# One decoder layer on one core: the hand-written order of every engine laid out anew

## What is computed

```python
# 1. linear attention with decay, 32 heads of 16
h = layernorm(x); xx = shifted(h) - h
r, k, v = (h + xx*maa_r) @ Wr.T + br, ..., ...
g = silu((h + xx*maa_g) @ Wg.T + bg)
y = ((r @ k) * Wm) @ v + (r @ state) * wb       # per head
x = x + ((headnorm(y) * ln_g + ln_b) * g) @ Wo.T + bo
# 2. cross attention: queries layernorm(x), keys and values ctx, 32 query and 8 key heads
x = x + softmax(q @ k.T / 4) @ v
# 3. feed-forward; every operand of both matmuls is rounded to 8 bits with one exponent per block of 32
h = mx_layernorm(bf16(layernorm(x)))
h = gelu(mx_quant(h) @ mx_quant(W1).T + b1)
x = x + bf16(residual + (mx_quant(h) @ mx_quant(W2).T + b2))
```

## Time and profile before

| what | value |
|---|---|
| median of 3 runs | 1534.97 us (1533.75 to 1541.5) |
| the profiled execution's own time | 1538.03 us |
| its span, first to last instruction | 1536.0 us |
| TensorE busy | 1297.9 us, 84% |
| VectorE busy | 1265.8 us, 82% |
| ScalarE busy | 773.2 us, 50% |
| GpSimd busy | 559.9 us, 36% |
| TensorE busy tenths, 40 slices of 38.4 us | 0004999999999999999999999999999999998743 |
| VectorE busy tenths | 3676647878899999999999998999999899887664 |
| granted clock of TensorE, mean | 0.974 |

### The profile page before, as it was taken

The page is one execution under the profiler, slowest core; times in us unless marked ns, Lnnn a source line. Parts: engine busy times, 40 slices in busy tenths (PEclk is TensorE's granted clock), DMA queues, the critical chain, the costliest instruction groups (busy, mean ns, idle before and its releaser), DMA issues.

```text
span 1536.0 us, 30462 instructions
## 1 busy us (share of the span) xinstructions
PE 1297.9 (84%) x11493; PEld 826.9 (54%) x11552; DVE 1265.8 (82%) x2092; ACT 773.2 (50%) x1611; POOL 559.9 (36%) x606
## 2 busy tenths in 40 slices
PE   0004999999999999999999999999999999998743
PEld 0003666556666666666666665666666666665311
DVE  3676647878899999999999998999999899887664
ACT  2002457556555555555555555665555555554340
POOL 2224333333344444443433343333444443433111
PEclk9999999999999999999999999999999999999766
DMA  7542000111111111111111111111111111111112
GB/s 284 121 98 47 9 8 14 35 36 33 26 36 34 27 23 27 35 34 35 34 34 34 35 34 34 34 34 28 34 35 22 21 35 34 35 32 29 25 25 44
DMA packets 150831, 62.76 MB, mean 41 GB/s; under 512 B 137632, under 2 KB 139040, under 8 KB 149920
## 3 DMA queue, kind: packets, MB, share of 16 engines
q1 hardware_dynamic: 150688, 60.83, 17.5%
HBM read 26.73 MB, written 8.39 MB: 23 GB/s over the span
## 4 chain that ended last, share of the span: by engine, by line
PE 32%; DVE 31%; issue 14%; DMA 9%; SPq 7%; ACT 6%; POOL 1%; DVEq 0%; POOLq 0%; ACTq 0%
PE bank_b L396 9%; DMA xin<-x 5%; PE rt L454 4%; SPq L214 4%; DVE att L1327 4%; DMA gmem<-w 3%; PE bank_y L419 2%; PE bank_o L480 2%; DVE amax_g L1400 2%; DVE mix_v L1304 2%; SPq L208 2%; PE bank_b L489 2%; PE bank_a L489 2%; PE bank_a L396 1%; PE rt L444 1%
## 5 line engine op out<-in xcount | busy, mean ns | idle before, releaser
L2880 POOL TENSOR_TENSOR x<-x,o_bf 128x512 f32<-128x512 f32 x32 | 37.2, 1162 | 488.6 <-DVE o_bf L1477 488.6
L1327 DVE TENSOR_TENSOR att<-rt,wm 128x2048 f32<-128x2048 f32 x64 | 146.3, 2286 | 5.1 <-PE bank_y L419 3.0
L1361 DVE TENSOR_REDUCE negm<-rt 128x16 f32<-128x2048 f32 x64 | 146.3, 2287 | 3.6 <-PE rt L454 2.1
L378 PE MATMUL bank_o<-ident,xx 128*128 128x128 f32 x128 | 20.4, 283 | 144.1 <-ACT xx L2244 143.6
L2875 POOL TENSOR_TENSOR gmem<-gmem,unit_g 128x1024 bf16<-128x1024 bf16 x64 | 124.5, 1945 | 47.2 <-DVE unit_g L1411 46.1
L500 PE MATMUL bank_y<-w2q,gmem 128*128 128x512 bf16 x511 | 118.9, 387 | 17.9 <-DMA gmem<-gmem 16.9
L2342 ACT ACTIVATE pT<-rt 128x2048 f32<-128x2048 f32 x64 | 119.5, 1868 | 14.1 <-PE rt L467 11.7
L396 PE MATMUL bank_b<-mix_k,w_Wk 128*128 128x128 f32 x1024 | 123.1, 280 | 3.5 <-DVE mix_k L1304 3.5
L396 PEld LDWEIGHTS bank_b<-mix_k,w_Wk 128*128 128x128 f32 x1024 | 121.4, 197 | 7.1 <-issue 3.8
L396 PE MATMUL bank_a<-mix_r,w_Wr 128*128 128x128 f32 x1024 | 122.6, 278 | 0.0
L433 PE MATMUL bank_y<-w_Wo,yT 128*128 128x512 f32 x256 | 120.5, 614 | 0.0
(11 more groups left out here) (171 smaller groups left out, 2938.1 us busy)
## 6 DMA issues: line engine op xcount, KB each, us to landing
xin<-x SPq DMA_DIRECT2D x32, 256.0 KB, 3.2
gmem<-w SPq DMA_DIRECT2D x16, 512.0 KB, 4.5
out<-x SPq DMA_DIRECT2D x32, 256.0 KB, 2.0
kv<-ctx SPq DMA_DIRECT2D x32, 64.0 KB, 3.1
w_Wv<-Wv SPq DMA_DIRECT2D x1, 1024.0 KB, 5.7
w_Wk<-Wk SPq DMA_DIRECT2D x1, 1024.0 KB, 8.6
w_Wr<-Wr SPq DMA_DIRECT2D x1, 1024.0 KB, 12.7
w_Wg<-Wg SPq DMA_DIRECT2D x1, 1024.0 KB, 14.8
```

The costliest lines, as they stand in the source:

```text
L1327: e.tensor_tensor(att[:, :, :, :, :].rearrange("p g m a t -> p (g m a t)"), rt[:, :], wm[:, i, :, :, :, :].rearrange("p g m a t -> p (g m ...
L1361: e.tensor_reduce(negm[:, 0:H].rearrange("p (g i j) -> p g i j", g=4, i=2)[:, :, i, :], rt[:, :].rearrange("p (g j s) -> p g j s", g=4, j= ...
```

## The change

Nothing that is computed changes but one thing: the gate's bias is added by ScalarE in four instructions (`gate_in`, a function of ScalarE now) and not by VectorE in one. Everything else is order. The 16 weight pieces stand between the steps of the first four sequences on VectorE, GpSimd and SyncE; the first loads come in another order; the loops run over `range(9, 28)` with another order inside, and the written-out starts and ends differ from before in many places.

```diff
@@ SyncE, the first loads
+            load_w12(0)
             load("Wv", wt["Wv"][:, :, :], weights["Wv"])
             load("dist", minus_dist, consts["minus_dist"])
             load("bv", row["bv"][:, :], rows["bv"])
...
             load_w12(1)
...
             load("b1", b1row[:, :], b1)
             for k in ROWS[1:]:
                 load("rows", row[k][:, :], rows[k])
+            load_x(1)
+            load("Wk", wt["Wk"][:, :, :], weights["Wk"])
+            load("faaaa", bonus[:, :], faaaa)
+            load("Wo", headmean[:, :], consts["headmean"])
+            load("Wo", wt["Wo"][:, :, :], weights["Wo"])
+            load("Wr", wt["Wr"][:, :, :], weights["Wr"])
+            load("Wg", wt["Wg"][:, :, :], weights["Wg"])
+            w12_turned(0)
             load_w12(2)
+            load_w12(3)
+            load_w12(4)
             w12_turned(1)
...
@@ VectorE
-            def gate_in(n):
+            def gate(n):
                 e.wait_ge(sem("act_gt"), n + 1)
-                if n:
-                    e.wait_ge(sem("dve_yT"), n)
-                e.tensor_tensor(gh[:, :, :], heads4(bank_b[:, :]), per_col(col["bg"]), ALU.add).then_inc(sem("dve_gh"), 1)
-
-            def gate(n):
-                e.wait_ge(sem("dve_gh"), n + 1)
+                e.wait_ge(sem("act_gh"), n + 1)
...
@@ ScalarE
+            def gate_in(n):
+                e.wait_ge(sem("pe_g"), n + 1)
+                if n:
+                    e.wait_ge(sem("dve_yT"), n)
+                for m in range(KT):
+                    done = e.activation(gh[:, m, :], bank_b[:, m * T:(m + 1) * T], ACT.Identity,
+                                        bias=col["bg"][:, m:m + 1])
+                done.then_inc(sem("act_gh"), 1)
...
@@ GpSimd, from the start
             w12_scaled(0)
+            mixed(0, "r")
             w12_scaled(1)
+            mixed(0, "g")
             w12_scaled(2)
+            mixed(1, "g")
+            mixed(1, "r")
             w12_scaled(3)
             w12_scaled(4)
+            gate_parts(0)
+            gate_rstd(0)
...
```

More of the change, by code:

```diff
@@ new lines, in _ @@
+            e.wait_ge(sem("dve_Ra1"), 27)
+            scores_x(25, 0)
+            e.wait_ge(sem("act_neg"), 26)
+            head_variance(26)
+            e.wait_ge(sem("act_rz"), 28)
+            project_v(27)
+            e.wait_ge(sem("act_ex0"), 26)
+            scores_x(25, 1)
+            e.wait_ge(sem("act_expv"), 53)
+            values_x(25, 0)
+            e.wait_ge(sem("dve_yz"), 27)
+            project_out(26)
+            e.wait_ge(sem("act_ex1"), 26)
+            scores_r(27, 0)
@@ L1551, in _ @@
+            stats_q(2)
+            spread_v(1)
+            norm_mv("q", 2)
+            w12_scale(8)
+            decayed(1, 1)
             w12_quantise(7)
-            means_removed()
-            w12_scale(8)
+            w12_quantise(8)
+            differences(2)
+            mixed(2, "k")
             w12_scale(9)
-            w12_quantise(8)
+            maxima(0, 0)
+            w12_scale(10)
             w12_quantise(9)
-            w12_scale(10)
+            maxima(0, 1)
+            gate(1)
@@ L2637, in _ @@
+            weights_x(25, 0)
+            keys_r(27)
             out_x(25, 0)
```

1767 lines of the change are left out of this document (861 added, 906 removed).

## The result

The changed kernel takes 1512.15 us (median of 4 runs, 1510.58 to 1513.42) against 1535.77 for the kernel before: a ratio of 0.984, 95% interval 0.9811 to 0.9869. It is faster, but by 24 us and not by the 67 forecast, and it lies outside the range of 1440 to 1496.

The account below looks back on a forecast made before the run. The prediction took the start to be bound by a chain of loads and VectorE's work, the loop by TensorE. 1538.0 - 53.6 (start) - 13.5 (loop) = 1470.9, with gate and drain 0; 1468 after 3.1 for median runs; range 1440 to 1496.

Parts of the forecast that it names:

- The start: Up to sequence 3, weight pieces between the sequences' steps: head_variance(3) 53.6 us earlier, at 223.
- The waits for the pieces' loads: VectorE in the start: 9 us at piece 2, 25 us over pieces 5 to 15 and what follows; before, 37.0.
- Rival A: In the start, the weight pieces stay a chain: 36 us gained there, 1485 us in all; chance 0.22 together with B.
- Rival B: In the start, TensorE runs at a slow clock: another 15 us, 1483 in all; chance 0.22 together with A.
- The gate: gate_in moved from VectorE to ScalarE: covered by other work, 0 us; up to 1.1 a sequence if not.
- The loop: Sequences 4 to 31: TensorE's waits shrink, 0.5 us faster a sequence, 13.5 us over 27 periods.
- The waits for `pT` and `xx`: TensorE in the loop, before the second scores_x and turn_x: 0.4 and 0.3 us a sequence, both should go.
- `mix_v` is free of GpSimd's product: VectorE in the loop: the mix of v took 2.8 us beside GpSimd's gmem multiplication, which is now done elsewhere.
- `down`: TensorE in the loop: starts 1 us earlier after project_out, three turnings still in a row; near zero, either sign.
- Rival E: In the loop, a smaller loss of D's kind, 1.1 us a sequence: 1511 us; chance 0.07.
- D: In the loop, the mix of r comes late, project("r") 2.3 us late each turn: 1543 us; chance 0.03.
- The drain: The last 110 us, from the last head_variance: keeps its chain, 0 us.

Follow-up runs that it names:

- e5_quant: The changed kernel with VectorE's gelu_quantised(.,0) back behind hidden_quantised in the loop, as in the kernel before: 1484.8 us.
- e3_turn: The changed kernel with SyncE turning the gelu's first half ahead of the hidden in the loop: 1483.5 us.
- e2_early: The changed kernel with gelu_pow2(.,1) back right behind gelu_max(.,1) in the loop, and GpSimd's gelu_scale(.,1) ahead of gate_rstd again: 1511.8 us.

## Why the prediction was right and wrong

**The start: right.** `decayed(3, 0)` was put at 194.3 and came at 191.2, `head_variance(3)` at 223 and came at 220.5; 53.6 us were forecast, 56.2 came. Its parts were less good. The waits for the pieces' loads were 16.6 us, where I had 29 (34 with the load of sequence 3 and `weighted(0)`), while waits that I had not named in the list took their place: 7.0 for the load of sequence 2 and some 14 for other engines, where I had allowed 10. So the sum came out near partly because its terms missed in opposite ways. The quantising of a piece was slowed beside GpSimd more rarely than before, and not more often as I had feared: of the even pieces the median is 1.23 us (the row below) and not 2.0, and of all 16 pieces 3 took over 1.9 us where 7 had. Rival A is out: the pieces are no chain. Rival B is out as a price: the granted clock was 0.88 up to the mark, between the two levels, and the mark still came early.

```profile
L1489 DVE SCALAR_TENSOR_TENSOR hz<-gmem,pow_w x8: 1224/1226/2817, 13.1 to 175.2; 128x1024 bf16<-128x1024 f32 x8
```

**The gate: right at 0 for the kernel before, wrong for this one.** In the old order the move is worth 3.8 us, near my 0. In the new one the same half on VectorE would stand between weight steps and hold `project("k")` of sequence 1 for 14.2 us. So some 18 of the start's 56 us hang on the gate, a term that I had put at 0. I costed the edits one by one against the old order, and they are not independent. How much of it is the place that I gave `gate_in` in that list was not tried.

**The loop: wrong, and this is the step that failed.** I wrote "I take 0.5 faster, nearer to the row of waits". It came 1.65 slower: 13.5 us were to be gained over 27 turns and 43.8 were lost over 28. I had read the waits of TensorE, seen that each could go, and taken what was left as a gain. The waits for `pT` and `xx` did go, though `turn_x` kept a wait of 0.3 us for another reason. What I had not done is walk VectorE's stretch from `second_out` to `yT`, as I had walked its list at the start. Here is its start, each wait in it and its end, first before, then after, in one turn of each:

```profile
746.58 0.68 DVE L1470 SCALAR_TENSOR_TENSOR o_bf<-bank_y,r_b 128x512 bf16<-128x512 f32 x1
...
748.52 0.98 DVE L1297 TENSOR_TENSOR xx<-xT 128x512 f32<-128x512 f32 x1 [0.20 <-ACT xT L2280]
...
753.00 0.26 DVE L1367 RECIPROCAL rden<-bank_o 128x16 f32<-128x16 f32 x1 [0.15 <-PE bank_o L480]
...
771.15 0.75 DVE L1395 SCALAR_TENSOR_TENSOR hz<-hw,rstd_g,r_ffn_ln_b 128x512 bf16<-128x512 f32 x1 [0.30 <-ACT rstd_g L2232]
...
773.99 0.69 DVE L1348 TENSOR_TENSOR yT<-yT,gh 128x512 f32<-128x512 f32 x1
```

```profile
751.06 0.68 DVE L1465 SCALAR_TENSOR_TENSOR o_bf<-bank_y,r_b 128x512 bf16<-128x512 f32 x1
...
753.50 1.22 DVE L1395 TENSOR_REDUCE amax_g<-gmem 128x32 f32<-128x1024 bf16 x1 [0.70 <-ACT gmem L2347]
...
755.60 0.42 DVE L1370 TENSOR_TENSOR x<-bank_o,rden 128x256 f32<-128x256 f32 x1 [0.36 <-DMA out<-x]
...
757.40 0.69 DVE L1297 TENSOR_TENSOR xx<-xT 128x512 f32<-128x512 f32 x1 [0.18 <-ACT xT L2261]
...
768.01 2.29 DVE L1327 TENSOR_TENSOR att<-rt,wm 128x2048 f32<-128x2048 f32 x1 [0.92 <-PE rt L406]
...
780.71 0.69 DVE L1343 TENSOR_TENSOR yT<-yT,gh 128x512 f32<-128x512 f32 x1
```

From the first start to the last end it is 28.1 us before (774.68 - 746.58) and 30.3 after (781.40 - 751.06). The waits are 0.65 before and 2.16 after, 1.5 more; work is 0.7 more, with `gelu_round` and `gelu_quantised` of the first half in it (1.45 us) and `gate_in` out of it. Before, TensorE came to `project_out` some 0.9 us after `yT` was there; that cover went first. The rest is TensorE's wait. That this stretch and the row of turnings set the turn, in rings that close from one turn to the next, is what `e5_quant` and `e3_turn` show: 1.3 and 1.5 us a turn back, each by one edit on one of the two.

My one argument for a gain there, that `mix_v` is free of GpSimd's product, was true (2.79 to 1.14 us), and the 1.7 us came back on `pow_h`. I had written that "GpSimd now does that multiplication elsewhere" and not asked where. `e2_early` shows that another place within the stretch is no better. The Trainium skill ("SBUF — State Buffer", section "SBUF: two separate sides") has the shared port pair as a lock for a whole instruction; the trace agrees, with 1.91 for 0.17 us.

For `down` I had the mechanism: it starts earlier, the three turnings stay in a row, "near zero, either sign". It waited 0.95 us.

**Rival E** took the slow end of the loop's estimate, where both places are named with 1 us each, and its 1511 is what was measured. I gave it 0.07. It calls itself of the same kind as D, whose late mix of `r` did not come: TensorE waits for it in no turn. Its sum was right partly by luck: it had 30 us lost where 43.8 were, and no gain in the drain where 14.3 came.

**The drain: wrong by 14.3 us, and not tested.** I took 0. The last `turn_out` starts 50.6 us after the last variance and not 59.3. Before, TensorE waited 4.5 us there for a turning in front of an `up`; now that `up` comes without a wait. The granted clock is 0.76 and not 0.70 over the drain, and TensorE's work there 6.1 us shorter. Which of these is cause was left open. All experiments on the changed kernel have drains of 96 to 104 us, the two on the kernel before 109.4 and 110.5, so it lies in the written-out end and not in the loop.

**Range and chances.** "Faster" was right. The range failed since its lower and upper ends came mainly from the start, the best known part; for the loop I had named ends from -0.85 to +1.1 us a turn, which is -23 to +30 us, and let only a part of them in.

## What to carry to other kernels

When a loop is laid out anew, price it by the rings that close from one turn to the next and not by the waits of the busiest engine. Walk each engine's stretch between two hand-overs, and add the DMAs that close the ring with all that stands ahead of them in their queue. A wait that only moves when its instruction moves may belong to a ring; look for the buffer or the queue place that cuts it. And edits that pay alone can undo each other: here two that brought 28 us each made 1517 us together, since one queued the finished hidden behind the half that the other made late.
